# A GNN's attention stage: the vector engine's unit loop turned to begin with the maxima, PE's sums drawn together, and records and edge features fetched earlier

## What is computed

```
def gcn_layer(h, W, b):                      # three times: 16 -> 64 -> 64 -> 16
    h = h @ W
    msg = norm[:, None] * h[row]
    return segment_sum(msg, col) + b
x = layernorm(x + gcn(x))

w_m = (efeat @ W_msg + b_msg).reshape(E, 16, 16)     # per edge
w_a = (efeat @ W_attn + b_attn).reshape(E, 16, 16)
h_src = feat[src][:, :, None]
e1, e2 = w_m * h_src, w_a * h_src
ex = exp(e2 - segment_max(e2, dst)[dst])
attn = ex / segment_sum(ex, dst)[dst]
x = layernorm(x + segment_sum(e1 * attn, dst).sum(axis=1))
```

## Time and profile before

| | us |
|---|---|
| median of 3 runs | 2584.24 |
| lowest, highest | 2573.64, 2599.27 |
| the profiled execution, its own time | 2582.71 |
| its span, first to last instruction | 2581.0 |

### The profile page before, as it was taken

How to read it: one execution, slowest core, us unless ns; L and a number is a source line. 1 busy time by engine, 2 the same in 40 slices (tenths; PEclk the granted TensorE clock), 3 DMA queues, 4 the chain that set the end, 5 groups by cost and what they waited for, 6 DMA issues and landing times.

```text
span 2581.0 us, 38167 instructions
## 1 busy us (share of the span) xinstructions
PE 1837.5 (71%) x5814; PEld 689.5 (27%) x5815; DVE 1990.6 (77%) x3249; ACT 1467.1 (57%) x5049; POOL 1344.3 (52%) x1593
## 2 busy tenths in 40 slices
PE   3666666689437777777777777777777777777755
PEld 1111111233302232323333223332233232233222
DVE  5999999731238888888877888887788888778756
ACT  5347612101137676767766667766667666667643
POOL 1424306655355665666655565655556556556540
PEclk9898988788659999999999999999989989899878
DMA  1010000000001000000000000000000000000000
GB/s 24 24 27 0 1 1 8 8 24 11 12 10 9 9 9 10 9 9 9 10 9 9 9 9 10 9 9 9 9 9 9 10 9 9 9 9 9 9 5 7
DMA packets 85438, 25.78 MB, mean 10 GB/s; under 512 B 61869, under 2 KB 82463, under 8 KB 85279
## 3 DMA queue, kind: packets, MB, share of 16 engines
q0 software_dynamic: 36672, 18.09, 5.9%
q1 hardware_dynamic: 45359, 6.52, 1.6%
q10 hardware_dynamic: 3376, 0.83, 0.2%
HBM read 22.74 MB, written 2.51 MB: 10 GB/s over the span
## 4 chain that ended last, share of the span: by engine, by line
PE 28%; issue 25%; DVE 23%; DVEq 14%; ACT 6%; another core or an unknown queue 2%; DMA 1%; ACTq 1%; SPq 0%; PEldq 0%; PEld 0%; POOLq 0%
PE pair L847 14%; DVE hot L1260 6%; ACT eo L1083 4%; DVE eo L1549 4%; PE pw L834 3%; DVE eo L1583 3%; DVEq L1568 2%; DVE eo L1592 2%; DVE top L1564 2%; PE pw L721 2%; PE pair L843 2%; PE pw L728 1%; PE pt L816 1%; PE pw L725 1%
## 5 line engine op out<-in xcount | busy, mean ns | idle before, releaser
L633 POOL DMA_INDIRECT nbr<-table,rec x928 | 947.9, 1021 | 610.6 <-ACT eo L1083 357.8
L847 PE MATMUL pair<-eo,ident 128*128 128x512 f32 x1856 | 909.4, 636 | 12.3 <-issue 7.6
L1083 ACT ACTIVATE eo<-pw,nbr 128x32 f32<-128x32 f32 x3712 | 697.5, 364 | 137.4 <-issue 119.7
L1549 DVE TENSOR_TENSOR eo<-pw,nbr 128x1024 f32 (+1 forms) x348 | 413.1, 1218 | 250.0 <-PE pw L834 106.0
L834 PE MATMUL pw<-wk,termsT 100*128 100x512 bf16 x928 | 299.7, 409 | 308.7 <-issue 223.3
L847 PEld LDWEIGHTS pair<-eo,ident 128*128 128x128 f32 x1856 | 371.8, 204 | 505.8 <-issue 490.1
L1059 ACT CAST termsT<-pt 100x512 bf16<-100x512 f32 x232 | 135.8, 585 | 278.4 <-issue 162.3
L1260 DVE TENSOR_SCALAR hot<-iota_key,near_key 128x500 bf16<-128x500 f16 x974 | 278.1, 347 | 14.1 <-issue 7.3
L1592 DVE TENSOR_TENSOR eo<-eo x232 | 272.5, 1215 | 5.7 <-ACT eo L1072 5.6
L1583 DVE TENSOR_TENSOR eo<-eo,bank (+1 forms) x116 | 265.3, 2287 | 10.7
L1072 ACT ACTIVATE eo<-eo 128x2048 f32<-128x2048 f32 x116 | 221.3, 1908 | 70.2 <-DVE eo L1583 44.6
(11 more groups left out here) (247 smaller groups left out, 1754.5 us busy)
## 6 DMA issues: line engine op xcount, KB each, us to landing
nbr<-table,rec POOLq DMA_INDIRECT x928
rec<-unit_recs SPq DMA_DIRECT2D x116, 8.0 KB
attr<-in_edge_attr_dram,rec POOLq DMA_INDIRECT x116
unit_recs<-place SPq DMA_DIRECT2D x27, 64.0 KB
shared<-key_row SPq DMA_DIRECT2D x1, 1600.0 KB, 6.4
counts<-in_dst_dram SPq DMA_DIRECT2D x1, 448.0 KB
counts<-in_src_dram SPq DMA_DIRECT2D x1, 448.0 KB
place<-in_src_dram,at_i POOLq DMA_INDIRECT x26, 2.7
```

Of the source, the lines that this page charges most:

```text
L633: pool.indirect_dma_start(nbr[:, b, j * FEAT:(j + 1) * FEAT], None, table, bass.IndirectOffsetOnAxis(ap=rec[:, b, j:j + 1], axis=0)).then_ ...
L847: mm = pe.matmul(total, ident[:], eo[:, ring, j * 2 * CH:(j + 1) * 2 * CH], start=False, stop=(j == SLOT - 1), skip_group_check=True)
L1083: done = act.activation(eo[:, ring, lo:lo + wide], pw[:, j - 4, c * wide:(c + 1) * wide], ACT.Copy, scale=nbr[:, held, j * FEAT + c:j * FE ...
L1549: dve.tensor_tensor(eo[:, bass.ds(ring, 1), k * 4 * CH:(k + 1) * 4 * CH] .rearrange("p r (c f) -> p (r c) f", f=2 * FEAT), pw[:, 2 * (k % ...
```

## The change

1. **DVE's loop is turned.** An iteration is now `peaks(v)`, `rest_two(v+3)`, `scaled(v+2)`, `accumulate(v-1)`, `weighted(v)`, `rest_one(v+4)`. With v = u+1 this is the old ring, cut at another place.
2. **A tile's first unit has its own text in `peaks`.** There the maximum of the unit is the running maximum, and `mdiff` is a memset. Elsewhere `mdiff` and the new maximum are two plain tensor_tensor operations, `mdiff` first. The running maximum lies in one fixed place, `bank[0][:, 0:256]`.
3. **`finished`** (reciprocal, product, reduction, with drains between) stands whole at the end of a tile's first iteration, no longer between the steps of `peaks`.
4. **PE: both halves of `sums` come before `product(u+3, 1)`.**
5. **Start of the unit loop.** Four records are loaded as soon as they are written; `rec` no longer shares space with the first part. Edge features of four units are gathered when PE is through the first part (`s_over`), before the table is there. SP waits for all four features first. `clear` does most memsets while ACT takes the layer norm's root. ACT does `high` and `middle` of units 2 and 3 before `last_pair(0)`, and DVE their rests before `scaled(0)`. `peaks(0)` comes before `scaled(1)`.

```diff
@@ SP
+            for b in range(SETS):
+                sp.dma_start(rec[:, b, :], unit_recs[:, b, :]).then_inc(s_rec[b], 16)
             sp.wait_ge(s_x1, 1)
             sp.dma_start(table[0:NG * P, :].rearrange("(t p) f -> p t f", p=P), x1[:]).then_inc(s_tab, 16)
-            sp.wait_ge(s_stage, 1)
-            for b in range(2):
-                sp.dma_start(rec[:, b, :], unit_recs[:, b, :]).then_inc(s_rec[b], 16)
...
+            for b in range(SETS):
+                sp.wait_ge(s_attr[b], 16)
+                sp.sem_inc(s_attr_ok, 1)
+            for b in range(SETS):
+                records(0, b, b >= 2, True)
@@ GpSimd
+            pool.wait_ge(s_over, 1)
+            for b in range(SETS):
+                gather_attr(b, b, 0)
             pool.wait_ge(s_pads, 16)
             pool.wait_ge(s_tab, 16)
-            pool.wait_ge(s_stage, 1)
...
+            for b in range(SETS):
+                gather_rows(b, b)
+            with pool.Fori(1, quads) as i:
                 for b in range(SETS):
...
+                    gather_attr(b, i * SETS + b, i)
+                    gather_rows(b, i * SETS + b)
@@ PE
+            pe.drain().then_inc(s_over, 1)
...
                 sums(b % RING, 0, u)
+                sums(b % RING, 1, u)
                 if ahead > 2:
                     product((b + 3) % 2, 1, u + 3)
-                sums(b % RING, 1, u)
@@ ACT
-            act.wait_ge(s_stage, 1)
+            act.wait_ge(s_ones, 1)
...
             for u in range(2):
                 high(u, u + 2, u + 2)
                 middle(u, u + 2)
+            for u in range(2):
                 last_pair(u, u, u)
                 for half in range(2):
                     turned(u, half, u + 2)
-            powers(0, 0)
+                if u == 0:
+                    powers(0, 0)
@@ DVE
+            def clear():
+                dve.wait_ge(s_over, 1)
+                dve.memset(terms[:, :, :, TERMS * FEAT:KROWS], 1.0).then_inc(s_ones, 1)
+                dve.memset(acc[:], 0.0)
+                dve.memset(pen[:, 0:1], -3e38)
+                dve.memset(pen[:, 1:2], 0.0)
+                dve.memset(bank[0][:], 0.0)
+            layernorm(x1, y3, 1, clear)
...
+            top_run = bank[0][:, 0:CH]
+            def peaks(ring, seen, place, low=None):
...
-                dve.drain()
-                dve.tensor_tensor(top1[:], top2[:, 0:CH], top2[:, CH:2 * CH], ALU.max)
-                if ended:
-                    outcome(*ended)
-                dve.drain()
-                dve.scalar_tensor_tensor(out=after, in0=before, scalar=pen[:, bass.ds(first, 1)], in1=top1[:],
-                                         op0=ALU.add, op1=ALU.max)
-                dve.scalar_tensor_tensor(out=mdiff[:], in0=before, scalar=pen[:, bass.ds(first, 1)], in1=top1[:],
-                                         op0=ALU.add, op1=ALU.subtract).then_inc(s_md, 1)
+                if place == "first":
+                    dve.memset(mdiff[:], -3e38).then_inc(s_md, 1)
+                dve.drain()
+                if place == "first":
+                    dve.tensor_tensor(top_run, top2[:, 0:CH], top2[:, CH:2 * CH], ALU.max)
+                else:
+                    dve.tensor_tensor(top1[:], top2[:, 0:CH], top2[:, CH:2 * CH], ALU.max)
+                    dve.drain()
+                    if place == "inner":
+                        dve.tensor_tensor(mdiff[:], top_run, top1[:], ALU.subtract).then_inc(s_md, 1)
+                        dve.tensor_tensor(top_run, top_run, top1[:], ALU.max)
...
+                peaks(here, v, place, low)
+                if ahead > 2:
+                    rest_two(odd, v + 3)
+                    scaled(third, third, v + 2)
+                accumulate(odd, dve.snap(v - 1, min_val=0, max_val=MANY))
+                weighted(here, v)
...
+                if ahead > 3:
+                    rest_one(even, here, v + LEAD)
+                if tile is not None:
+                    finished(tile, odd)
```

More of the change, by code:

```diff
@@ L324, in gnn_kernel @@
         s_stage = sem("s_stage")
+        s_over = sem("s_over")
+        s_ones = sem("s_ones")
         s_hi = sem("s_hi")
@@ L1553, in scaled @@
                                       ALU.mult).then_inc((s_pair0_free, s_pair1_dve, s_scaled)[k], 1)
-            def peaks(ring, first, old, new, seen, ended=None):
+            top_run = bank[0][:, 0:CH]
+            def peaks(ring, seen, place, low=None):
                 def wide(v):
                     return v.rearrange("p (c o) -> p c o", o=FEAT)
-                before = bank[0][:, bass.ds(old, CH)]
-                after = bank[0][:, bass.ds(new, CH)]
                 dve.wait_ge(s_pair1_act, seen + SETS + 1)
@@ L1625, in _, with finished @@
                 dve.drain()
+            for u in range(2):
+                rest_one(u, u + 2, u + 2)
+                rest_two(u, u + 2)
+                dve.drain()
+            dve.drain().then_inc(s_attr_free, 3)
+            def finished(tile, unit):
+                inverse(tile, unit)
+                dve.drain()
+                quotient(tile, unit)
+                dve.drain()
+                outcome(tile, unit)
             scaled(0, 0, 0)
-            rest_one(0, 2, 2)
-            rest_two(0, 2)
@@ L1629, in _ @@
             dve.drain()
+            peaks(0, 0, "first")
             scaled(1, 1, 1)
-            rest_one(1, 3, 3)
-            rest_two(1, 3)
-            dve.drain().then_inc(s_attr_free, 3)
             scaled(2, 2, 2)
-            peaks(0, 0, CH, 0, 0)
-            left = dve.alloc_register("dve_left")
-            dve.reg_mov(step, 0)
+            dve.sem_inc(s_tile, 1)
+            dve.drain()
+            weighted(0, 0)
+            rest_one(0, 0, LEAD)
+            dve.reg_mov(step, 1)
@@ L1677, in _, with one_unit @@
[L1677 to L1682 removed]
+            def one_unit(place, tile=None, ahead=LEAD, load=None, low=None):
+                v = dve.snap(step, min_val=1, max_val=MANY)
+                even = dve.snap(v % 2, min_val=0, max_val=1)
+                odd = dve.snap((v + 1) % 2, min_val=0, max_val=1)
+                here = dve.snap(v % RING, min_val=0, max_val=RING - 1)
+                third = dve.snap((v + 2) % RING, min_val=0, max_val=RING - 1)
+                peaks(here, v, place, low)
[4 more added lines that the diff above has]
+                weighted(here, v)
+                if load is not None:
+                    dve.reg_mov(units, dve.value_load(levels[0:1, bass.ds(load, 1)], min_val=1, max_val=E))
+                if ahead > 3:
+                    rest_one(even, here, v + LEAD)
+                if tile is not None:
+                    finished(tile, odd)
+                dve.reg_add(step, step, 1)
@@ L1683, in _ @@
+            with dve.Fori(1, dve.snap(units, min_val=1, max_val=E)):
+                one_unit("inner")
+            with dve.Fori(1, NT - 1) as t:
+                one_unit("first", t, load=t)
+                with dve.Fori(1, dve.snap(units, min_val=1, max_val=E)):
+                    one_unit("inner")
+            dve.reg_mov(units, dve.value_load(levels[0:1, NT - 1:NT], min_val=3, max_val=E))
             n = dve.snap(units, min_val=3, max_val=E)
             some = dve.alloc_register("dve_some")
-            dve.reg_sub(left, n, 3)
@@ L1694, in _ @@
-            one_unit(None, None, 1)
-            one_unit(None, None, 0)
+                    one_unit("inner")
+            one_unit("either", dve.snap(within + (NT - 1), min_val=NT - 1, max_val=NT), 3, low=pen[:, bass.ds(within, 1)])
+            one_unit("inner", None, 1)
+            one_unit("inner", None, 0)
+            dve.wait_ge(s_sum, dve.snap(step, min_val=1, max_val=MANY))
+            dve.sem_inc(s_settled_dve, 1)
             total = dve.snap(step, min_val=1, max_val=MANY)
```

108 lines of the change are left out of this document (34 added, 74 removed).

## The result

| | us | runs |
|---|---|---|
| kernel before, median | 2589.11 | 2573.64 to 2599.27 (4) |
| changed kernel, median | 2501.96 | 2484.33 to 2524.87 (4) |
| ratio | 0.9646 | 95% interval 0.9565 to 0.9726 |
| forecast | 2350 | 2290 to 2490 |

The change is faster, by 3.5% and not by 9%; the time lies above the range. The ratio is one of means and leaves out the run of 2524.87 us, whose granted clock was the lowest of the four. The profiled execution took 2501.98 us, span 2500.2. Against the 2581.0 before, the 80.8 us come from three places: the second unit's first maximum 771.44 to 754.68 (-16.8), from there to the last one 1772.7 to 1707.5 (**-65.2, where 207 were forecast**), and +1.2 behind it.

The account below looks back on a forecast made before the run. The prediction took a closed cycle through ACT's `last_pair` and PE's product and sums to bound most units. From 2582.7 us it took 207 for the loop and 25 for the start: 2351, rounded to 2350, range 2290 to 2490.

Parts of the forecast that it names:

- What a unit will take: Unit loop: DVE 12.4 us, three other engines about 11 to 12; with 0.4 us of waits, 12.8 us a unit.
- Rival 1: Unit loop: gathers become the limit part of the time, 3.7 us lost in every third unit, 2490 us; chance 0.15.
- The ring: Unit loop: `last_pair`, 3.9 us of product and sums, transposes, casts, back to `last_pair`; longer than DVE's work in most units.
- sums first: PE in the unit loop: putting both halves of the sums ahead takes product and second half, 3.9 us, out of the cycle.
- `peaks` by 0.4 us: DVE in an inner unit: two replacement operations shorten `peaks` by 0.4 us, leaving 12.4 us of work a unit.
- A tile's first unit, net nothing: 24 such units: about 0.6 us saved in `peaks` is offset by `finished` standing whole; 16.2 us each.
- Start, -25: Start of the unit loop: early edge features bring the second unit's first maximum to 746; gain 25 us, between 10 and 36.
- End, 0: Last units and final norm: they keep their work, so 0 us.
- 2: Unit loop: slower, a 3.7 us stall in every unit, 16.5 us a unit, 2773 us; chance 0.06.
- 3: GpSimd: DVE's three maxima block it as `weighted` does, the loop keeps 15.5 us a unit, 2558 us; chance 0.03.
- 4: PE: the new order brings nothing, the wait moves to pair 1 at a lower TensorE clock, 2514 us; chance 0.08.
- 5: Whole change: it does not do what it says, only the early features could be late, 2376 us; chance 0.02.

Follow-up runs that it names:

- e16: Changed kernel with `last_pair` as 48 activations instead of 32, on chip 12: 2353.26 us, 1.0203 of the kernel before.
- e5: Changed kernel, nothing edited, run again on chip 5: 2278.9 us, 0.988 of the kernel before.
- e7: Changed kernel with `last_pair` as 48 activations instead of 32, on chip 8: 2576.82 us, 1.0337 of the kernel before.
- e8: Kernel before with `last_pair` as 48 activations instead of 32, on chip 8: 2925.27 us, 1.1715 of the kernel before.
- e2: Kernel before with only PE's new order, both halves of the sums ahead of product 1, on chip 0: 2332.58 us, 1.009 of the kernel before.
- e6: Kernel before, nothing edited, run again for its profile on chip 5: 2306.29 us, ratio 0.9991.
- e11: Changed kernel with GpSimd waiting after each unit's eight row gathers until they have landed, on chip 15: 2449.82 us, 1.061 of the kernel before.
- e17: Changed kernel, nothing edited, run again on chip 12: 2280.61 us, 0.9888 of the kernel before.
- the wide `last_pair`: Changed kernel with `last_pair` as 16 activations of 64 columns, every second scale left out: 0.9909 to 0.9923 of the kernel before.
- e15: Kernel before with `last_pair` as 48 activations instead of 32, on chip 4: 2912.26 us, 1.1688 of the kernel before.

## Why the prediction was wrong

**The step that failed** is *What a unit will take*: "Four engines within half a microsecond or so of each other do not all run at their best, so I leave 0.4 us of waits a unit ... and take 12.8". ACT's share in it, "about 11 to 12", was a sum of durations with `last_pair` at its even pace. In the profiled pair it did not keep that pace: 6.48 us before, 7.52 after. ACT's ring then took 14.2 us in the unit shown, and without seven long units inner ones came to 13.7 on the mean instead of 12.8, tile-first ones to 17.4 instead of 16.2. With 86 and 21 of them that is 76 + 25 = 101 us; the seven long units took 66 us more than forecast, and the 25 us kept for one long wait near the end did not come: 142 us, the loop's whole miss. The 119.7 us of "issue" at the activations, 1.0 us a unit, lay open in the page before, in the row of `last_pair`; the sum has no term for them.

ACT's pace is not the whole of it. In e16 `last_pair` takes as long as in the profiled pair, 7.56 us against 7.52, with every start in time; the median unit there is 13.24 us, against 13.64 in the profiled pair and 12.29 where `last_pair` takes 5.3. By that estimate ACT's pace stands for 0.95 of 1.35 us. The rest is not assigned. Part of it may be PE's term, which also grew: from second to last maximum PE is busy 1398.1 us at a granted clock of 0.87, against 1290.9 at 0.95 in e5, with the same matmuls.

**Rival 1 came true in part, with another cause.** The seven units of 21.3 to 25.8 us cost some 59 us over their neighbours. Five of them lie where GpSimd issued 17 gathers or more without a pause, as foreseen, and a sixth where its last gathers run into 24 writes; the loop's other four such stretches lie at units of 17.2 to 17.9 us, where the median is 13.6. But e5 shows longer stretches that hold up nobody, and in e7 starts are late without any such stretch in the loop. Gathers and late instructions coincide in the profiled pair; neither is shown to cause the other. That this rival's time, 2490, lies near the measured one is luck: it wanted 140 us from such units.

**The ring was real and the 3.9 us were not its price.** Where `last_pair` is long, the kernel without sums first stands at 18.9 us a unit and the one with it at 14.8 (e8, e7; these differ in `peaks` and the rest too, and sums first was not run by itself there). Where instructions come in time and `last_pair` is short, it is worth 0.7% beside the rest of the change and costs 1% by itself. What I had named as late next, product 1 behind 7.2 us of sums, is what it costs. The prediction had PE "finished both halves about when ACT is done"; by its own rows, 1624.7 + 7.2 = 1631.9 against 1629.45, PE is 2.5 us late, and 3.2 were measured in e2.

***`peaks` by 0.4 us*: right, as far as it was tested.** It was not run by itself. On chip 5 the commonest inner unit goes from 12.70 to 12.29 us. The 12.8 forecast for the mean is 12.57 there; only the unit of before was 12.81 already.

***A tile's first unit, net nothing*: nearly.** 15.11 to 15.60 on chip 5, 24 times 0.5 us, with the small waits inside `finished` (0.29 and 0.17 us) that the old text covered.

***Start, -25*: right in kind, -16.8.** `high` and `middle` of all four units were done early, but `last_pair(0)` took 16 us and the loop began behind it. In e5 it is -20.7 against e6. ***End, 0*: right**, +1.2.

**The other rivals.** 2 needed a stall in every unit; there was none. 3: the price did not come, the gathers mean 1.030 us after and 1.021 before, but that the maxima do not hold GpSimd up is wrong. The one gather in the earlier trace rows was no fair sample: 17 before and 18 after took over 1.2 us with no `weighted` beside them. This one of the changed kernel begins just inside the first maximum and ends with the second:

```profile
882.21 1.23 DVE L1593 TENSOR_TENSOR top<-eo 128x1024 f32 x1
882.31 1.94 POOL L632 DMA_INDIRECT attr<-in_edge_attr_dram,rec  x1 [0.30 <-issue]
883.53 0.69 DVE L1596 TENSOR_TENSOR top<-top 128x512 f32<-128x512 f32 x1
```

4: the wait did not move to pair 1, but what I held against it failed too: from second to last maximum the granted clock fell from 0.93 to 0.87 instead of rising. e11, where only a pause of GpSimd was added and the clock of the same stretch is 0.87 as well (0.94 in e17), shows that waiting by itself goes with a lower clock. 5: the order of the sums shows that the change was made.

*Open:* what makes instructions late, on which chips, and whether fewer of them or pauses of GpSimd would help there, and whether the 3.5% come again there; the wide `last_pair` was run on four chips and the pause on two, and on none of them was anything late. The Trainium skill (Runtime: NRT & Kernel Launch, "Instruction fetch mechanics") says that each engine's sequencer fetches ahead by its own queue, and that this is mostly hidden. On five chips the traces agree: `last_pair` has 1.0 us of waits in 3712 activations (e6). If the late starts are late fetches, which no run here shows, then the first pair's traces don't: 119.7 and 202.1 us in the same instructions.

## What to carry to other kernels

Read the "issue" time inside a run of equal, independent instructions first: 0.17 us apart and then 0.7 is no wait of the program, and a sum of durations must take that engine at the pace it shows, not at its even one. Before costing a change by the waits of one profile, see whether they are the kernel's: here 203 of 209 us were gone when the same kernel was profiled again. "Issue" is not proof of a late instruction either: compare the row's start with the end of what it needs (385 of 434.9 us in e15 were a wait for `last_pair`). A change that takes work away from the engine that a unit waits for shows in the unit (0.4 us of `peaks` on chip 5); one that shortens a ring pays only where the ring is what a unit waits for, and can cost elsewhere (1% in e2).

## What the runs showed of the hardware

The same program took 2589 us in the first pair, 2496 and 2497 on chips 8 and 4, and 2306 to 2310 on chips 0, 5, 12, 13 and 15, at a granted clock of 0.90 to 0.93 in all of them. In the slower profiles small activations on ACT start about 0.70 us apart, or 1.2 to 1.4, once mostly 19 to 31 of them have started 0.17 us apart, and waits on PE and DVE end long after what they wait for (9 us for DVE at 724.46). In the kernel before, 16 more activations a unit cost 430 us of 2496 (e8), ring and late instructions together; in the changed one 73 of 2281 where they are in time (e16 against e17).

A gather that begins beside DVE's first maximum can last until the second has ended (1.94 us at 882.31, against 0.94 for most).
